# A fused attention and mixture kernel: first attention with two row tiles, joined latent weights, and the output's moments by the aggregate instruction

## The chip, the cores and the metric

One core of one Trainium2 chip runs the whole program in one launch. The metric is the device time of one execution in microseconds (us). TensorE is written PE (PEld is its weight load), VectorE DVE, ScalarE ACT, GpSimd POOL, SyncE SP. SBUF is the memory beside the engines, PSUM the one that PE writes, here 8 banks of 512 float32 columns.

## What is computed

All arrays are float32. Over 32 entries of 128 tokens x 128 features (x) with 120 context rows each, five stages run one after the other:

```
1 l0 attention: kv_in = [LN(ctx); LN(x)] (248 rows), q = LN(x) Wq, k,v = kv_in Wkv   (8 heads of 64)
                q, k are divided by their length per head; masked softmax of 8 q.k; y = (p v) Wo
                x = x + LN(y) w + b
2 l0 ffn:       up to three steps relu(x Wm^T) * active, Wp^T, with a choice of 512 columns between steps
3 l1 attention: 16 heads of 8, keys and values from ctx (120 rows)
4 mla:          16 heads of 8: q = h Wq, c = h Wdkv (64 wide), k = c Wuk, v = c Wuv, causal softmax, Wo
5 moe:          8 experts, the best two per token, silu(t w1) w2
```

## The kernel before, in words

Each stage is a function with one program per engine; engines meet only at semaphores, and each engine works off its own list in order. In the attention stages every engine runs a `body(n)` for each entry n, in which the work of entries n-1, n, n+1 and n+2 is interleaved by hand. That order is all there is of a schedule.

Stage 1 is `l0_attention`, with `softmax_units` for its softmax: eight heads are handled as two units u of four heads; a unit's scores fill two PSUM banks (2u and 2u+1), two heads of 248 columns in each. The steps of one entry m:

- DVE normalizes x and ctx (L650, L652), PE turns both (L474, L475), ACT copies them into `kvT`. PE projects q, kc (keys of ctx) and kl (keys of x) (L481, L482, L487); ACT copies each into `qk` (L586) and squares all (L591); DVE sums the squares (L657, L662); POOL takes the power -1/2 (L742, `r_norm`) and multiplies (L745, `qkn`). That POOL product is signalled as `normed`.
- PE turns `qkn` (L494, L498, L504); ACT and DVE copy it to `KT` and `QZ`. `QZ` holds, for each head, a 128-row tile of which 64 rows stay zero, so that a product over all 128 rows gives the score of one head (L384). The mask enters each bank as a product of `first_row` and `keep_row` (L380).
- DVE takes the maximum (L162), ACT the exponentials (L171), PE turns the probabilities (L184, L190), ACT and DVE copy them (L196, L201). DVE inverts the sums (L177) and spreads them (L414, `r_wide`), PE turns them (L421), ACT copies them (L428). PE multiplies by the values (L436, L438), DVE scales (L447), PE projects (L453), ACT copies `y` (L606).
- For y, DVE takes statistics (L675) and six small operations (L678 to L687), POOL the power (L751), DVE normalizes (L692), POOL weighs, biases and adds (L755 to L760), DVE takes the statistics of x (L697).

`copy_qk(m)` on ACT may overwrite `qk` only when `normed` has counted entry m-1, so the chain copies, kl projection, copy, squares, sums, power, product closes on itself once per entry. In bodies, `copy_qk(n + 2)` follows the exponentials of unit 1 of entry n.

In the mla stage (`attention16`, kind mla), PE makes the 64-wide latent c (L1405), ACT copies it (L1510), and PE makes keys and values from it (L1418, L1419), placed between `turn_group(n, par, 0)` and `turn_group(n, par, 1)`; `scores(n + 1)` (L1431 bias, L1436) come right after.

## Time and profile before

| | us |
|---|---|
| median of 3 runs | 1520.29 (1519.94 to 1520.65) |
| profiled execution, its own time | 1520.62 |
| its span, first to last instruction | 1518.9 |
| mean granted PE clock over the span | 0.942 of full speed |
| stage 1, to its last DVE row | 0 to 579.6 |
| stage 4 (mla) | about 1011 to 1266 |

Times in rows are us from the start of the span, except mean durations, which are in ns. The profile merges neighbouring instructions of a line ("x4"); a matmul of float32 is two instructions in the records, one for each part of the numbers.

### The profile page before, as it was taken

The page shows a single profiled execution, that of the slowest core. Times are in us where ns is not written, and L with a number is a line of the kernel's source. Part 1 is how long each engine was busy: PE and PEld are TensorE (multiplying, and loading weights), DVE is VectorE, ACT ScalarE, POOL GpSimd, SP SyncE. Part 2 cuts the span into 40 slices and gives each one's busy share as a digit, 9 for nine tenths or more (in the row PEclk, how much of TensorE's full clock was granted, in tenths as well). Part 3 has the DMA queues.
Part 4 walks back from the last instruction along what each step waited for, and adds up shares of the span by engine and source line. Part 5 has one row for each costly group of instructions (what it writes and reads, how often), then busy time and mean ns, then how long its engine had stood idle before and what let it go on. Part 6 is the DMA issues. An engine that isn't in the chain of part 4 may idle for free. (4 is left out here: it accounts for less than half of the span.)

```text
span 1518.9 us, 38140 instructions
## 1 busy us (share of the span) xinstructions
PE 1320.3 (87%) x13781; PEld 963.8 (63%) x13781; DVE 1031.7 (68%) x2266; ACT 759.3 (50%) x2067; POOL 559.6 (37%) x546
## 2 busy tenths in 40 slices
PE   1699999999999996931389988969999997999998
PEld 0377676776776773421277676747878885777776
DVE  5377777777777773767388888868999995343432
ACT  1467767767767661300155555536666663333332
POOL 3556555555555543000221222234222222334333
PEclk9899999999999997965599999988999998999999
DMA  7000000000000000000000000010000000000000
GB/s 200 0 1 0 0 0 0 0 0 0 0 0 0 0 1 0 0 1 0 9 11 7 8 8 8 7 57 2 1 0 0 0 2 1 8 8 14 7 7 14
DMA packets 22727, 14.56 MB, mean 10 GB/s; under 512 B 6377, under 2 KB 21609, under 8 KB 22538
## 3 DMA queue, kind: packets, MB, share of 16 engines
q1 hardware_dynamic: 22520, 13.75, 3.5%
q8 instruction: 37, 0.61, 0.2%
q14 instruction: 24, 0.20, 0.0%
q10 hardware_dynamic: 146, 0.01, 0.0%
HBM read 11.66 MB, written 2.10 MB: 9 GB/s over the span
## 5 line engine op out<-in xcount | busy, mean ns | idle before, releaser
L742 POOL TENSOR_TENSOR r_norm<-ssm,mhalf 128x24 f32<-128x24 f32 x32 | 133.6, 4176 | 176.1 <-DVE ssm L662 176.1
L171 ACT ACTIVATE l_probs<-psum,l_n_max 128x248 f32<-128x248 f32 x256 | 117.0, 481 | 101.4 <-DVE l_n_max L162 101.4
L1845 ACT ACTIVATE hid<-psum 128x512 f32<-128x512 f32 x128 | 76.3, 597 | 136.3 <-PE psum L1793 136.3
L1906 DVE TENSOR_TENSOR prod<-psum,combine 128x512 f32<-128x512 f32 x64 | 44.2, 691 | 143.9 <-PE psum L1803 143.9
L1803 PEld LDWEIGHTS psum<-w,hid 128*128 128x128 f32 x1024 | 123.1, 192 | 26.8 <-issue 26.8
L1937 POOL TENSOR_TENSOR acc<-acc,prod 128x512 f32<-128x512 f32 x64 | 81.1, 1268 | 146.9 <-DVE prod L1906 146.9
L384 PE MATMUL psum<-KT,QZ 128*128 128x248 f32 x512 | 128.4, 373 | 0.0
L1803 PE MATMUL psum<-w,hid 128*128 128x128 f32 x1024 | 123.4, 275 | 0.0
L1793 PE MATMUL psum<-moe_hT,w 128*128 128x512 f32 x256 | 122.0, 605 | 0.0
L384 PEld LDWEIGHTS psum<-KT,QZ 128*128 128x128 f32 x512 | 98.1, 192 | 18.9 <-issue 0.7
L1658 POOL TENSOR_TENSOR l_QX<-l_qT,l_own_slots 128x512 f32<-128x512 f32 x32 | 33.3, 1040 | 185.1 <-ACT l_qT L1504 178.5
L745 POOL TENSOR_TENSOR qkn<-qk,r_norm 128x1536 f32<-128x1536 f32 x32 | 88.4, 2762 | 3.6 <-POOL r_norm L742 2.2
L1658 POOL TENSOR_TENSOR mla_QX<-mla_qT,mla_own_slots 128x512 f32<-128x512 f32 x32 | 33.3, 1040 | 149.5 <-ACT mla_qT L1504 149.5
L1380 ACT COPY l_probsT<-psum 120x512 f32<-120x512 f32 x64 | 37.5, 585 | 100.4 <-PE psum L1446 100.4
L162 DVE TENSOR_REDUCE l_n_max<-psum 128x4 f32<-128x992 f32 x64 | 75.7, 1183 | 8.8 <-PE psum L384 8.8
L1446 PE MATMUL psum<-ident,mla_probs 128*128 128x128 f32 x512 | 76.2, 283 | 1.5 <-ACT mla_probs L1524 1.3
L657 DVE TENSOR_REDUCE ss<-sq 128x24 f32<-128x1536 f32 x32 | 56.1, 1753 | 30.1 <-ACT sq L591 30.1
L1524 ACT ACTIVATE mla_probs<-psum,mla_n_max 128x128 f32<-128x128 f32 x256 | 69.5, 382 | 13.9 <-DVE mla_n_max L1558 13.9
L201 DVE COPY l_probsT<-psum 128x512 f32<-128x512 f32 x64 | 43.9, 685 | 41.6 <-PE psum L190 41.6
L1446 PE MATMUL psum<-ident,l_probs 128*120 128x128 f32 x512 | 70.5, 281 | 0.0
L1524 ACT ACTIVATE l_probs<-psum,l_n_max 128x120 f32<-128x120 f32 x256 | 68.0, 385 | 5.0 <-DVE l_n_max L1558 5.0
L586 ACT COPY qk<-psum 128x512 f32<-128x512 f32 (+1 forms) x96 | 54.5, 619 | 30.6 <-PE psum L487 22.7
(307 smaller groups left out, 3458.8 us busy)
## 6 DMA issues: line engine op xcount, KB each, us to landing
X<-x_in SPq DMA_DIRECT2D x8, 256.0 KB, 4.9
out_dram<-acc SPq DMA_DIRECT2D x32, 64.0 KB, 1.5
CT<-ctx_in SPq DMA_DIRECT2D x8, 240.0 KB, 6.2
l_cT<-ctxT_in SPq DMA_DIRECT2D x32, 60.0 KB, 1.8
w<-w_in SPq DMA_DIRECT2D x1, 1024.0 KB, 4.9
wm<-wm_in SPq DMA_DIRECT2D x1, 768.0 KB, 4.6
wp<-wp_in SPq DMA_DIRECT2D x1, 768.0 KB, 6.7
wkv<-wkv_in SPq DMA_DIRECT2D x1, 512.0 KB, 5.1
```

What stands on the lines that cost most here:

```text
L162: dve.tensor_reduce(n_max[u][:, :].rearrange("p (c j) -> p c j", c=2), psum[:, 2 * u:2 * u + 2, 0:HB * K].rearrange("p c (j k) -> p c j k" ...
L171: e = act.activation(probs[u][:, h, :], psum[:, 2 * u + h // HB, (h % HB) * K:(h % HB + 1) * K], ACT.Exp, bias=n_max[u][:, h:h + 1], accum ...
L384: mm = pe.matmul(psum[:, 2 * u + c, j * K:(j + 1) * K], QZ[par][:, h, :], KT[par][:, h // 2, :], start=False, stop=True, skip_group_check= ...
L742: pool.tensor_tensor(r_norm[:, :], ssm[:, :], mhalf[:, 0:3 * H], ALU.pow).then_inc(s["norm_inverted"], 1)
L745: pool.tensor_tensor(qkn[:, :, :].rearrange("p a (h d) -> p (a h) d", d=HD), qk[:, :, :].rearrange("p a (h d) -> p (a h) d", d=HD), r_norm ...
L1446: tr = pe.transpose(psum[0:K, 4 + g % 2, j * P:(j + 1) * P], probs[par][:, 4 * g + j, :], ident[:, :])
L1524: e = act.activation(probs[par][:, h, :], psum[:, h // 4, (h % 4) * K:(h % 4 + 1) * K], ACT.Exp, bias=n_max[par][:, h:h + 1])
L1658: pool.tensor_tensor(QX[par][:, :, :], qT[:, :].unsqueeze(1).broadcast_to([P, 4, P]), own_slots[:, :].unsqueeze(2).broadcast_to([P, 4, P]) ...
L1793: pe.matmul(psum[:, 2 + i % BANKS, :], w1[:, e, half * P:(half + 1) * P], hT[par][:, :], start=True, stop=True).then_inc(hidden[i], 1)
L1803: mm = pe.matmul(psum[:, 5 + e % 2, b * D:(b + 1) * D], hid[i % RING][:, b * P:(b + 1) * P], w2[:, i, :], start=(half == 0), stop=(half == ...
L1845: act.activation(hid[i % RING][:, :], psum[:, 2 + i % BANKS, :], ACT.Silu).then_inc(activated[i], 1)
L1937: pool.tensor_tensor(a[:, :, :], a[:, :, :], prod[e % 2][:, :, :], ALU.add).then_inc(summed[e], 1)
```

## The change

It has five parts.

1. Stage 1, scores: q is kept compact in `QT` (64 rows for each head, two heads above each other), and two heads are multiplied at a time, one on array rows 0 to 63 and one on 64 to 127, each into its own bank. The mask is given at rows 0 and 64, from a small tile `keep_now` that POOL copies for each entry. The value products are written down in another order (context part of two heads, then x part of the two).
2. Stage 1, order: `softmax_units` and `run_entries` go, and every engine gets a new `body`, run by `run_steps` from n = -2 to 33 (a step is skipped where its entry does not exist). The old bodies are printed above, the new ones stand in the diff.
3. Stage 1, moments of y: `bn_aggr` gives mean and variance at once, and one addition of epsilon follows.
4. Stage 1, scales of the later entries (two powers over 28 columns each, L119) are cut into four pairs over 7 columns.
5. Stage 4: Wdkv Wuk and Wdkv Wuv are multiplied once in the stage's setup (`joined`), and q, k, v come straight from the input in one step `project_qkv`. Stage 3 gets the same step with its own weights.

```diff
-        QZ = [sb(f"QZ{i}", [P, H, P]) for i in range(2)]
+        QT = [sb(f"QT{i}", [P, 4, P]) for i in range(2)]
+        keep_now = [sb(f"keep_now{i}", [P, K], BF16) for i in range(2)]
...
-                act.dma_start(keep8[:, :], keep_in).then_inc(keep_loaded, 16)
+                for r in (0, 64):
+                    act.dma_start(keep8[r:r + 1, :], keep_in).then_inc(keep_loaded, 16)
...
-                dve.tensor_scalar(keep_row[0:1, :, 0:C], keep8[:, :].rearrange("a (b c) -> a b c", b=B), 1.0, -NEG_MAX,
-                                  ALU.subtract, ALU.mult)
+                for r in (0, 64):
+                    dve.tensor_scalar(keep_row[r:r + 1, :, 0:C], keep8[r:r + 1, :].rearrange("a (b c) -> a b c", b=B), 1.0, -NEG_MAX,
+                                      ALU.subtract, ALU.mult)
...
-            dst, src = QZ[par][r, half:H:2, :], psum[r, 7, :].rearrange("p (c q) -> p c q", c=4)
+            dst, src = QT[par][r, :, :], psum[r, 7, :].rearrange("p (c q) -> p c q", c=4)
...
-            pe.matmul(psum[:, 2 * u + c, 0:2 * K], first_row[:, :], keep_row[:, entries(n), :].broadcast_to([P, 2, K]),
-                      start=True, stop=False, skip_group_check=True)
-            for j in range(2):
-                h = 4 * u + 2 * c + j
-                mm = pe.matmul(psum[:, 2 * u + c, j * K:(j + 1) * K], QZ[par][:, h, :], KT[par][:, h // 2, :],
-                               start=False, stop=True, skip_group_check=True)
...
+                def scores(n, u, par):
+                    if there(n):
+                        if u == 0:
+                            wait(pe, s["qT_copied"], n + 1)
+                            wait(pe, s["qT_scaled"], n + 1)
+                            wait(pe, s["klT_copied"], n + 1)
+                            wait(pe, s["keep_copied"], n + 1)
+                        wait(pe, exp_done[u], n)
+                        for r in range(2):
+                            pe.matmul(psum[:, 2 * u + r, 0:2 * K], first_row[64 * r:64 * r + 64, :],
+                                      keep_now[par][64 * r:64 * r + 64, :].unsqueeze(1).broadcast_to([64, 2, K]),
+                                      start=True, stop=False, skip_group_check=True)
+                        for j in range(2):
+                            for r in range(2):
+                                mm = pe.matmul(psum[:, 2 * u + r, j * K:(j + 1) * K], QT[par][64 * r:64 * r + 64, 2 * u + j, :],
+                                               KT[par][64 * r:64 * r + 64, 2 * u + j, :], start=False, stop=True,
+                                               skip_group_check=True)
+                        mm.then_inc(scored[u], 1)
...
-            for j in range(4):
-                h = 4 * u + j
-                o = psum[HD * (j % 2):HD * (j % 2) + HD, 5, (j // 2) * P:(j // 2 + 1) * P]
-                pe.matmul(o, VC[par][0:C, h * HD:(h + 1) * HD], probsT[u][0:C, 0, j, :], start=True, stop=False,
-                          skip_group_check=True)
-                mm = pe.matmul(o, VL[par][:, h * HD:(h + 1) * HD], probsT[u][:, 1, j, :], start=False, stop=True,
-                               skip_group_check=True)
-            mm.then_inc(pv_done[u], 1)
...
+                        for j in range(2):
+                            for part, V, rows in ((0, VC, C), (1, VL, P)):
+                                for r in range(2):
+                                    h = 4 * u + 2 * j + r
+                                    mm = pe.matmul(psum[HD * r:HD * r + HD, 5, j * P:(j + 1) * P], V[par][0:rows, h * HD:(h + 1) * HD],
+                                                   probsT[u][0:rows, part, 2 * r + j, :], start=(part == 0), stop=(part == 1),
+                                                   skip_group_check=True)
+                        mm.then_inc(pv_done[u], 1)
...
+                def body(n, par):
+                    values_x(n + 1)
+                    scores(n, 1, par)
+                    project(n - 1)
+                    turn_inputs(n + 2)
+                    turn_probs0(n, 0)
+                    turn_probs1(n, 0)
+                    project_kc(n + 2)
+                    turn_sums(n, 0)
+                    project_q(n + 2)
+                    multiply_v(n, 0, par)
+                    turn_probs0(n, 1)
+                    turn_kc(n + 1)
+                    project_kl(n + 2)
+                    turn_probs1(n, 1)
+                    turn_kl(n + 1)
+                    turn_q(n + 1)
+                    multiply_v(n, 1, par)
+                    turn_sums(n, 1)
+                    values_c(n + 2)
+                    scores(n + 1, 0, 1 - par)
...
+                def copy_part(m, part, proj, copied, bank, rows):
+                    if there(m):
+                        wait(act, s["normed"], m)
                         wait(act, s[proj], m + 1)
-                        act.copy(qk[0:rows, i, :], psum[0:rows, bank, :]).then_inc(s[copied], 1)
...
+                def body(n, par):
+                    copy_values_c(n + 1, 1 - par)
+                    exponentials(n, 0)
+                    take_projection(n - 1)
+                    make_kvT(n + 2)
+                    copy_pt0(n, 0)
+                    copy_values_x(n + 1, 1 - par)
+                    exponentials(n, 1)
+                    copy_sums(n, 0)
+                    copy_part(n + 2, 1, "kc_proj", "kc_copied", 6, C)
+                    copy_part(n + 2, 0, "q_proj", "q_copied", 7, P)
+                    copy_pt0(n, 1)
+                    copy_kcT(n + 1, 1 - par)
+                    copy_part(n + 2, 2, "kl_proj", "kl_copied", 7, P)
+                    square_qk(n + 2)
+                    copy_qT(n + 1, 1 - par)
+                    copy_sums(n, 1)
...
-                    dve.tensor_tensor(y_sums[:, :], y_stat[:, 1:3], y_stat[:, 4:6], ALU.add)
-                    dve.tensor_tensor(y_diff[:, :], y_stat[:, 1:2], y_stat[:, 4:5], ALU.subtract).then_inc(s["y_aggr"], 1)
-                    wait(dve, s["y_aggr"], n + 1)
-                    dve.tensor_scalar(y_mean[:, :], y_sums[:, 0:1], 0.5, None, ALU.mult)
-                    dve.tensor_scalar(y_within[:, :], y_sums[:, 1:2], 1.0 / D, LN_EPS, ALU.mult, ALU.add)
-                    dve.scalar_tensor_tensor(y_between[:, :], y_diff[:, :], 0.25, y_diff[:, :], ALU.mult,
-                                             ALU.mult).then_inc(s["y_parts"], 1)
-                    wait(dve, s["y_parts"], n + 1)
-                    wait(dve, s["y_inverted"], n)
-                    dve.tensor_tensor(y_var[:, :], y_within[:, :], y_between[:, :], ALU.add).then_inc(s["y_var_ready"], 1)
...
+                        wait_apart(dve, s["y_stats"], n + 1, s["ln_made"])
+                        dve.bn_aggr(y_moment[:, :], y_stat[:, :]).then_inc(s["y_aggr"], 1)
+                        wait(dve, s["y_aggr"], n + 1)
+                        wait(dve, s["y_inverted"], n)
+                        dve.tensor_scalar(y_var[:, :], y_moment[:, 1:2], LN_EPS, None, ALU.add).then_inc(s["y_var_ready"], 1)
...
+                def body(n, par):
+                    norm_inputs(n + 2)
+                    maximum(n, 1)
+                    invert_sums(n, 0)
+                    y_moments(n - 1)
+                    copy_pt1(n, 0)
+                    scale_out(n, 0)
+                    invert_sums(n, 1)
+                    copy_pt1(n, 1)
+                    copy_kl(n + 1, 1 - par)
+                    copy_qT(n + 1, 1 - par)
+                    sum_squares(n + 2)
+                    y_normalize(n - 1)
+                    maximum(n + 1, 0)
+                    scale_out(n, 1)
+                    x_moments(n - 2)
...
+                def copy_keep(m, par):
+                    if there(m):
+                        wait(pool, scored[1], m - 1)
+                        pool.tensor_copy(keep_now[par][:, :], row(keep_row, m)).then_inc(s["keep_copied"], 1)
...
+                def body(n, par):
+                    weigh(n - 2)
+                    copy_keep(n + 2, par)
+                    invert_deviation(n - 1)
+                    add_to_x(n - 2)
+                    invert_norms(n + 2)
+                    norm_qk(n + 2)
+                    later_scales(n)
...
+            wdkvT = sb("wdkvT", [LAT, D])
+            joined = sb("joined", [D, 2, D])
+            w_turned, w_copied, w_joined = sem("w_turned"), sem("w_copied"), sem("w_joined")
         with nc.Block() as block:
+            if not l1:
+                @block.tensor
+                def _(pe):
+                    pe.transpose(psum[0:LAT, 6, 0:D], wdkv[:, :], ident[:, :]).then_inc(w_turned, 1)
+                    pe.wait_ge(w_copied, 1)
+                    pe.matmul(psum[:, 7, 0:D], wdkvT[:, :], wk[:, :], start=True, stop=True)
+                    pe.matmul(psum[:, 7, D:2 * D], wdkvT[:, :], wv[:, :], start=True, stop=True).then_inc(w_joined, 1)
+                @block.scalar
+                def _(act):
+                    act.wait_ge(w_turned, 1)
+                    act.copy(wdkvT[:, :], psum[0:LAT, 6, 0:D]).then_inc(w_copied, 1)
+                    act.wait_ge(w_joined, 1)
+                    act.copy(joined[:, :, :], psum[:, 7, 0:2 * D].rearrange("p (w d) -> p w d", w=2))
...
-                def project_q(m):
+                def project_qkv(m, par):
                     if there(m):
                         wait(pe, z_copied, m + 1)
-                        if not l1:
-                            pe.matmul(psum[0:LAT, 7, 2 * P:3 * P], wdkv[:, :], zT[:, :], start=True, stop=True)
-                        pe.matmul(psum[:, 7, P:2 * P], wq[:, :], zT[:, :], start=True, stop=True).then_inc(q_proj, 1)
-                def project_kv(m, par):
-                    if there(m):
                         if l1:
                             wait(pe, c_loaded[par], (m - par) * 8 + 16)
-                            source = cT[par]
-                        else:
-                            wait(pe, lat_copied, m + 1)
-                            wait(pe, q_copied, m + 1)
-                            source = latT
-                        at = 2 * P if l1 else 0
-                        pe.matmul(psum[:, 7, at:at + K], wk[:, :], source[:, :], start=True, stop=True)
-                        pe.matmul(psum[0:K, 7, 3 * P:4 * P], source[:, :], wv[:, :], start=True, stop=True).then_inc(kv_proj, 1)
+                        pe.matmul(psum[:, 7, P:2 * P], wq[:, :], zT[:, :], start=True, stop=True)
+                        source = cT[par] if l1 else zT
+                        pe.matmul(psum[:, 7, 2 * P:2 * P + K], wk[:, :] if l1 else joined[:, 0, :], source[:, :], start=True, stop=True)
+                        pe.matmul(psum[0:K, 7, 3 * P:4 * P], source[:, :], wv[:, :] if l1 else joined[:, 1, :],
+                                  start=True, stop=True).then_inc(qkv_proj, 1)
                 def scores(n, par):
...
-                    project_q(n + 1)
+                    project_qkv(n + 1, 1 - par)
                     for g in range(4):
                         multiply_v(n - 1, 1 - par, g)
                     turn_group(n, par, 0)
-                    project_kv(n + 1, 1 - par)
                     turn_group(n, par, 1)
...
-                    copy_latent(n + 1)
```

## Rows read from the trace of the kernel before

**Rows 1.** Windows: busy PE, PEld, DVE, ACT, POOL, clock, DMA share, GB/s.

```profile
200.00:300.00 100.00, 99.87 (x634) 70.00 (x634) 73.28 (x160) 69.76 (x196) 54.14 (x39) 1.00 0.00 0
```

**Rows 2.** Timeline of PE and ACT in stage 1: start, duration, line, shape.

```profile
319.89 0.38 PE L380 MATMUL psum<-keep_row,first_row 128*128 x1
320.12 1.00 PE L384 MATMUL psum<-KT,QZ 128*128 128x248 f32 x4
...
323.50 0.47 ACT L171 ACTIVATE l_probs<-psum,l_n_max 128x248 f32<-128x248 f32 x1 [3.12 <-DVE l_n_max L162]
...
324.09 1.05 PE L453 MATMUL psum<-wo,outT 128*128 128x128 f32 x8
...
325.28 0.28 ACT L606 COPY y<-psum 128x128 f32<-128x128 f32 x1
...
328.10 0.45 PE L436 MATMUL psum<-l_probsT,VC 120*64 120x128 f32 x4
...
329.18 1.12 PE L481 MATMUL psum<-wq,kvT 128*128 128x512 f32 x2
```

**Rows 3.** Timeline of POOL, second and last product (29 entries apart).

```profile
83.93 2.76 POOL L745 TENSOR_TENSOR qkn<-qk,r_norm 128x1536 f32<-128x1536 f32 x1
...
553.27 2.76 POOL L745 TENSOR_TENSOR qkn<-qk,r_norm 128x1536 f32<-128x1536 f32 x1
```

**Rows 4.** Timeline from one product to the next power.

```profile
72.08 1.07 ACT L586 COPY qk<-psum 128x512 f32<-128x512 f32 x2 [3.18 <-POOL qkn L745]
...
73.88 0.58 ACT L586 COPY qk<-psum 128x512 f32<-128x512 f32 x1 [0.73 <-PE psum L487]
74.31 0.69 DVE L201 COPY l_probsT<-psum 128x512 f32<-128x512 f32 x1 [2.12 <-PE psum L190]
...
76.12 1.50 ACT L591 ACTIVATE sq<-qk 128x1536 f32<-128x1536 f32 x1
77.65 1.75 DVE L657 TENSOR_REDUCE ss<-sq 128x24 f32<-128x1536 f32 x1 [0.79 <-ACT sq L591]
...
79.69 4.16 POOL L742 TENSOR_TENSOR r_norm<-ssm,mhalf 128x24 f32<-128x24 f32 x1 [7.65 <-DVE ssm L662]
```

**Rows 5.** The page's costliest groups: busy us, mean ns, idle before.

```profile
L162 DVE TENSOR_REDUCE l_n_max<-psum 128x4 f32<-128x992 f32 x64 | 75.7, 1183 | 8.8 <-PE psum L384 8.8
```

**Rows 6.** DVE beside the POOL product of a later entry.

```profile
326.79 2.76 POOL L745 TENSOR_TENSOR qkn<-qk,r_norm 128x1536 f32<-128x1536 f32 x1 [0.16 <-POOL r_norm L742]
...
327.56 0.28 DVE L675 BATCH_NORM_STATS2 y_stat<-y 128x6 f32<-128x128 f32 x1
327.87 1.69 DVE L678 TENSOR_TENSOR y_sums<-y_stat 128x2 f32<-128x2 f32 x1
```

**Rows 7.** Instructions of two tiles: count, min/median/max ns, first and last start.

```profile
L414 DVE COPY r_wide<-l_r_sums x64: 293/294/2789, 65.6 to 570.7; 128x256 f32<-128x256 f32 x64
...
L1865 DVE TENSOR_SCALAR hn<-X,rms x32: 273/276/1326, 1271.9 to 1466.1; 128x128 f32 x24, 128x128 f32<-128x128 f32 x8
```

**Rows 8.** Timeline of PE in one mla entry.

```profile
1150.92 1.17 PE L1436 MATMUL psum<-mla_kT,mla_QX 32*128 32x128 f32 x32
...
1152.03 0.49 PE L1466 MATMUL psum<-mla_wo,mla_outT 128*128 128x128 f32 x2
...
1152.46 1.04 PE L1446 MATMUL psum<-ident,mla_probs 128*128 128x128 f32 x8
...
1153.43 0.43 PE L1405 MATMUL psum<-mla_zT,mla_wdkv 128*64 128x128 f32 x2
```

**Rows 9.** Longest waits in mla, 1060 to 1240: total, times, longest.

```profile
DVE mla_n_max L1558 <- PE psum L1436: 8.5, 24, 0.4
```

**Rows 10.** Setup, first entry and end of stage 1.

```profile
21.13 2.14 DVE L331 TENSOR_SCALAR keep_row<-keep 1x3840 bf16<-1x3840 uint8 x1
...
41.09 2.76 POOL L745 TENSOR_TENSOR qkn<-qk,r_norm 128x1536 f32<-128x1536 f32 x1
...
579.34 0.29 DVE L697 BATCH_NORM_STATS2 stats<-X 128x6 f32<-128x128 f32 x1 [1.70 <-POOL X L760]
```

More of the change, by code:

```diff
@@ L220, in l0_attention, with there @@
+def there(n):
+    return not isinstance(n, int) or 0 <= n < B
 def l0_attention(nc, psum, X, stats6, mean, rstd, mhalf, small, ident, ident_bf, ones, cols,
@@ new lines, in project @@
+                def project(n):
+                    if there(n):
+                        wait(pe, out_scaled[1], n + 1)
+                        for c in range(4):
+                            mm = pe.matmul(psum[:, 5, 0:D], outT[:, c, :], wo[:, c, :], start=(c == 0), stop=(c == 3))
+                        mm.then_inc(s["projected"], 1)
+                def body(n, par):
[19 more added lines that the diff above has]
+                    scores(n + 1, 0, 1 - par)
@@ L578, in make_kvT @@
-                    act.activation(kvT[:, C:K], psum[:, 6, P:2 * P], ACT.Identity, bias=LNL_B,
-                                   scale=LNL_W).then_inc(s["kvT_made"], 1)
-                def copy_qk(m):
-                    wait(act, s["normed"], m)
-                    for i, (proj, copied, bank, rows) in enumerate((("q_proj", "q_copied", 7, P), ("kc_proj", "kc_copied", 6, C),
-                                                                    ("kl_proj", "kl_copied", 7, P))):
+                    if there(m):
+                        wait(act, s["ln_turned"], m + 1)
+                        wait(act, s["vc_proj"], m)
+                        wait(act, s["vl_proj"], m)
+                        act.activation(kvT[:, 0:C], psum[:, 6, 0:C], ACT.Identity, bias=LNX_B, scale=LNX_W)
+                        act.activation(kvT[:, C:K], psum[:, 6, P:2 * P], ACT.Identity, bias=LNL_B,
+                                       scale=LNL_W).then_inc(s["kvT_made"], 1)
@@ new lines, in exponentials @@
+                def exponentials(n, u):
+                    if there(n):
+                        wait(act, max_taken[u], n + 1)
+                        wait(act, pt1_turned[u], n)
+                        wait(act, pt0_turned[u], n)
+                        wait(act, sum_inverted[u], n)
+                        for h in range(4):
+                            e = act.activation(probs[u][:, h, :], psum[:, 2 * u + h // 2, (h % 2) * K:(h % 2 + 1) * K], ACT.Exp,
+                                               bias=n_max[u][:, h:h + 1], accum_out=sums[u][:, h:h + 1])
+                        e.then_inc(exp_done[u], 1)
```

662 lines of the change are left out of this document (259 added, 403 removed).

## The prediction, written before the changed kernel was run

> **What bounds the kernel now.** I read the windows first. In stage 1 PE is recorded busy 99.87 us of 100 while ACT, DVE and POOL have 70, 73 and 54 [rows 1]. In mla DVE waits for nothing but 0.35 us of scores an entry (8.5 us in 24) [rows 9], so there it is DVE that is near its limit. The timeline of stage 1 then gives the period of an entry: the POOL product starts at 83.93 and, 29 entries later, at 553.27 [rows 3], so one entry takes 469.34 / 29 = 16.18 us. The reader should see in it which work PE spends: the scores of an entry run from 319.89 to 324.09, 4.2 us, four banks of 1.05 [rows 2]. So a cut of PE's work moves the period, until another chain sets it. The first product starts at 41.09 [rows 10], 42.8 us before the second; two periods would be 32.4, so 10.5 us are lost in the start. Stage 1 ends at 579.6 [rows 10].
>
> **Scores on two row tiles.** A bank costs a mask of 0.23 us (320.12 - 319.89) and four records of two heads, (1.05 - 0.23) / 4 = 0.21 each [rows 2]. If the two tiles run together, a unit costs 0.23 + 4 x 0.21 = 1.07 instead of 2.10. That they do run together is shown in mla: 32 records of 128 columns on four row tiles take 1152.03 - 1150.92 = 1.11 us, while eight transposes of 128 columns one after the other take 1153.43 - 1152.46 = 0.97, so 0.11 to 0.12 each [rows 8]; 32 in turn would need 3.5. The switch of tile shape costs something: eight records at 0.11 are 0.87, the next shape starts at 0.97, so 0.1 is left for a switch. Each of the two units now stands between full-array work on both sides, four switches, 0.4. PE saves 4.2 - 2 x 1.07 - 0.4 = 1.7 us an entry. The Trainium skill (TensorEngine Tiling (Array Packing), Tiling Modes, Key Properties) says that a change of tiling mode drains the engine; by that rule four more drains speak against the change, and this trace agrees on a cost, of about 0.1 us. By a free switch the saving would be 2.1, by the row 1.7. Bounds: no overlap at all gives -0.4 (a loss), full overlap with free switches 2.1; I take 1.7, since the mla row is the same kind of product.
>
> **Value products.** Sixteen records of 128 columns take 329.18 - 328.10 = 1.08 us [rows 2], where one after the other at 0.11 they would take 1.76. They overlap already, and the new writing order brings 0, at best 1.08 - 0.9 = 0.2 a unit.
>
> **What PE's own list then allows.** 16.18 - 1.7 = 14.5 us if all its present gaps stay, about 13.7 if the gaps of some 0.8 us close (my estimate from a walk along the list). Now the other chains count, and the new order decides them.
>
> **The chain of the norms.** ACT may copy `qk` only after `normed` of the entry before. In the new order it is: the product ends, ACT copies kc and q (1.07 for two), projection of kl until its copy starts (73.88 - 72.66 = 1.2, where 72.66 is the end of the first of the two copies), copy 0.58, squares 1.50, sums and the clamp until the power starts 79.69 - 77.65 = 2.04 [rows 4], power to product 4.34, product 2.76 [rows 6]. That is 13.5; DVE takes the turned q ahead of the sums (0.25), signals 0.1: 13.9 us. The closed chain is a floor that the old order did not reach.
>
> **ACT's list.** From the copy of kc: 4.4 us to the end of the squares (1.07 + 1.2 + 0.58 + 1.50), DVE's sums and clamp to 6.7, y normalized and the maximum of unit 0 (1.18 [rows 5]) to 8.2. Then four exponentials take 325.28 - 323.50 = 1.78 [rows 2], to 10.0, y copied at 10.5 once PE has projected (0.28 [rows 2]), then two halves of kvT, two copies like that of kl, exponentials 1.78 and the copied sums, together 3.8 by my estimate: 14.3 us until kc can be copied again. Without further trouble the period is max(13.7 to 14.5, 13.9, 14.3) = 14.3.
>
> **The port that DVE and POOL share.** While the product runs on POOL, some DVE operations stand still. `y_sums` starts at 327.87 and ends with the product at 329.55, taking 1.69 instead of 0.16 [rows 6]; `r_wide`, a copy inside SBUF, once took 2789 ns instead of 294, and `hn`, a multiplication by a scale, 1326 instead of 276 [rows 7]. The statistics of y, started at 327.56 in the midst of it, took their usual 0.28 [rows 6]. So a DVE operation with two SBUF inputs, or a simple SBUF copy or scaling, waits until the product ends; statistics do not. By the list above, DVE reaches the moments of y at about 11.3 of a period, and the product runs from 11.1 to 13.85: inside. `bn_aggr` I take as free like the statistics (0.2). The last step, the addition of epsilon to a 128x1 column, is a tensor_scalar from SBUF to SBUF, the form of `hn`. Its cost is between 0.15 and the rest of the product, 2.4. The nearest row says that it waits, and I take that. The Trainium skill (SBUF — State Buffer, which ops grab the shared pair) lists tensor_scalar among the operations that may take two ports; whether one with a single element per partition does, no row here shows.
>
> What is late next: `copy_pt1(n, 0)` is queued behind it on DVE, PE waits with the value products of unit 0, and behind those, in order, stand the turn of unit 1's probabilities, the turn of kc and the projection of kl. The chain closes through the product: copy 0.69 [rows 4], values 1.08 [rows 2], eight transposes 0.88 [rows 8], projection 1.2, copy 0.58, squares 1.50, sums 2.04 [rows 4], power 4.34, product 2.76 [rows 6], with five signals of about 0.1: **15.5 us**. ACT's list and PE's list fit into that.
>
> **Moments of y, masks, scales.** Five small DVE operations go, besides the wait in `y_sums`, off the path. POOL copies a mask of 248 columns each entry; its product over 1536 columns takes 2.76 [rows 6], so that is well under 1 us, and POOL is idle 46% of the time [rows 1], mostly ahead of the power: 0. The powers over 28 columns leave the start; the first interval becomes about one period. The setup gets a second `keep_row` operation of 2.14 us on DVE [rows 10], of which 0.4 to 2.1 is seen, and kc is projected ahead of q (0.9): the first product ends near 45.9 instead of 43.85. After the last product (556.0) 23.6 us follow today; 21.5 by the shorter list.
>
> Stage 1 then ends at 45.9 + 31 x 15.5 + 21.5 = 547.9, that is 31.7 us less.
>
> **Joined latent weights.** PE loses the latent product (two records, about 0.35 us [rows 8]) and two changes of tile shape, 0.5 in all; ACT loses a copy. The scores can start 0.5 earlier. DVE waits for them 0.35 us an entry [rows 9] and has no other gap, so the gain ends there: 31 x 0.3 = 9 us, from 0 to 11. The joint weights are made on idle PE and ACT beside 5 us of DVE work in the setup: 0; uncovered it would be 3. Stage 3 changes by 0: its PE asks for the same data in nearly the same order.
>
> **Sum.** 1518.9 - 31.7 - 9 = 1478.2 of span. The profiled execution took 1520.62, 1.7 more than its span and 0.3 more than the median; so 1478.2 + 1.7 - 0.3 = 1479.6, **1480 us**. Its own range is 1470 to 1490 (15.2 to 15.8 us an entry).
>
> **Rivals.**
> - *The small addition does not wait for the port.* Period 14.3: stage 1 ends at 45.9 + 443.3 + 21.5 = 510.7, so 68.9 + 9 less: **1442 us**. For it: one element per partition gains nothing from two ports. Against: `y_sums`, two elements, waited. With 13.9 to 14.8 it is 1430 to 1458.
> - *The row tiles do not overlap, or the parts of the float32 products run in turn.* PE has then 16.18 + 0.4, less gaps of 0.8: about 15.9. Stage 1 ends at 560, **1492 us**. The change would not do what it says, and the new order alone would pay. The mla row speaks against it. The same time comes if `r_wide` of unit 0, 0.4 us ahead of the product in my walk, slips behind its start.
> - *Slower.* The lock puts the whole product on the path: `r_wide` waits from its start, PE stands at `turn_sums`, and nothing behind it makes the time up. The period is 14.3 + 2.76 = 17.1, stage 1 ends at 597, **1529 us**. It decides from a period of (579.6 + 9 - 45.9 - 21.5) / 31 = 16.8 on. Against it: PE has other work to catch up with.
> - *Mla gains nothing* is inside each range (9 us).
>
> **Chances.** Addition waits 0.48, does not wait 0.34, no overlap or a late `r_wide` 0.11, slower 0.05, no change 0.02. The range 1434 to 1500 holds the first wholly, nearly all of the second and the third. Faster by over 0.2% is 0.93, within 0.2% (3 us, about what a measurement of this kernel can tell from none) 0.02, slower 0.05.
>
> **What would show it.** The spacing of the L745 products: 15.5, against 14.3 and 15.9. The duration of the small addition after `bn_aggr`: over 1 us or 0.15. The start of neighbouring score records: in pairs, and a unit of about 1.1 us. In mla, the wait of the maximum for PE: near 0, and a period shorter by 0.3. The prediction is wrong if DVE reaches the moments outside of the product, or if a chain that I did not walk (the first exponentials behind the sums on DVE) is longer than its rows.

## The result and the profile after

| | before | after |
|---|---|---|
| median | 1520.39 us (4 runs, 1519.94 to 1520.65) | 1445.07 us (4 runs, 1443.46 to 1447.12) |
| span of the profiled execution | 1518.9 | 1445.4 |
| stage 1 ends | 579.6 | 515.5 |
| two entries of mla, start to start | 14.70 | 13.79 |

The ratio is 0.9506, 95% interval 0.9489 to 0.9522: faster by 75 us. That lies in the predicted range (1434 to 1500), but not in the likeliest case (1480, itself 1470 to 1490). It is the first rival, "the small addition does not wait for the port", which gave 1442. The two profiled spans differ by 73.5 us: 64.1 in stage 1, 15 in mla, and the other stages together 5.6 longer in this execution.

Of the 64 us in stage 1, 51.6 are the period (29 entries of 1.78 us). Another 13.8 lie between the first POOL product and the third (42.8 us before, 29.0 after), against a first product that comes 2.3 us later. The prediction expected that first gain too. All runs below that start from the changed kernel keep most of it, so a run with nearly the old period can still be faster than the kernel before: old_order is by 25 us, 15 of them in mla. No run takes the new start back alone.

The timeline of POOL, third and last product of the changed kernel, 29 entries apart (against [rows 3]):

```profile
72.41 2.76 POOL L691 TENSOR_TENSOR qkn<-qk,r_norm 128x1536 f32<-128x1536 f32 x1
...
490.14 2.76 POOL L691 TENSOR_TENSOR qkn<-qk,r_norm 128x1536 f32<-128x1536 f32 x1
```

One entry takes (490.14 - 72.41) / 29 = **14.40 us**, where it took 16.18. The windows of 200 to 300 us, columns as in [rows 1]:

```profile
200.00:300.00 100.00, 99.95 (x722) 64.83 (x722) 69.94 (x145) 79.20 (x215) 62.94 (x50) 1.00 0.00 0
```

PE has almost no recorded gap (99.95 us busy of 100), as before; ACT does more in the same time (79 against 70 us). DVE has fewer busy us per 100 (70 against 73) although more entries pass: the wait inside `y_sums` and the small operations behind it are gone. The timeline of POOL and DVE shows the disputed addition (L645):

```profile
302.86 2.76 POOL L691 TENSOR_TENSOR qkn<-qk,r_norm 128x1536 f32<-128x1536 f32 x1
...
302.96 0.18 DVE L642 BATCH_NORM_AGGREGATE y_moment<-y_stat 128x2 f32<-128x6 f32 x1
303.18 0.15 DVE L645 TENSOR_SCALAR y_var<-y_moment 128x1 f32<-128x1 f32 x1
303.26 0.69 DVE L626 COPY l_probsT<-psum 128x512 f32<-128x512 f32 x1
```

DVE does reach the moments inside the product, as the walk said. But the addition takes 0.15 us there and the copy of unit 0's probabilities follows at once. In [rows 6] `y_sums` stood until the product's end.

The timeline of PE, the two units of scores around the value projection:

```profile
311.97 0.38 PE L386 MATMUL psum<-keep_now,first_row 64*128 64x496 bf16 x2
312.19 1.00 PE L391 MATMUL psum<-KT,QT 64*128 64x248 f32 x8
313.12 1.12 PE L375 MATMUL psum<-wkv,kvT 128*128 128x512 f32 x2
314.18 0.38 PE L386 MATMUL psum<-keep_now,first_row 64*128 64x496 bf16 x2
...
315.33 1.16 PE L444 MATMUL psum<-wo,outT 128*128 128x128 f32 x8
316.32 0.27 PE L322 MATMUL psum<-ident,ln_c 120*128 120x120 f32 x1
```

A unit takes 313.12 - 311.97 = 1.15 us with its switch (2.10 in [rows 2]): the row tiles run side by side.

### The profile page after: what moved, and what is told of

It reads as the page before. It is cut to its first block and busy times, and to the rows that moved or that the text cites. A ratio compares the mean times of both kernels' runs of the same rounds, so it can differ in the third digit from the quotient of the medians.

```text
span 1445.4 us, 38156 instructions
## 1 busy us (share of the span) xinstructions
PE 1241.4 (86%) x13722; PEld 888.8 (61%) x13722; DVE 974.8 (67%) x2140; ACT 766.0 (53%) x2037; POOL 569.5 (39%) x582
## 5 line engine op out<-in xcount | busy, mean ns | idle before, releaser
L634 DVE TENSOR_TENSOR outT<-psum,r_spread 128x256 f32<-128x256 f32 x64 | 26.9, 420 | 78.8 <-PE psum L435 73.3
L1396 PE MATMUL psum<-ident,mla_probs 128*128 128x128 f32 x512 | 69.8, 280 | 1.2 <-ACT mla_probs L1465 1.0
L1733 PEld LDWEIGHTS psum<-moe_hT,w 128*128 128x128 f32 x256 | 45.3, 195 | 35.8 <-issue 35.3
L1339 DVE COPY mla_probsT<-psum 128x512 f32<-128x512 f32 x96 | 62.8, 682 | 2.3 <-PE psum L1396 2.3
```

Of the source, the lines that this page charges most:

```text
L1339: copy(probsT[0:K, g, :, :], psum[0:K, 4 + g % 2, :].rearrange("k (j q) -> k j q", j=4)).then_inc(copied[g], 1)
L1396: tr = pe.transpose(psum[0:K, 4 + g % 2, j * P:(j + 1) * P], probs[par][:, 4 * g + j, :], ident[:, :])
L1733: pe.matmul(psum[:, 2 + i % BANKS, :], w1[:, e, half * P:(half + 1) * P], hT[par][:, :], start=True, stop=True).then_inc(hidden[i], 1)
```

## The experiments

Each changes one thing in the changed kernel, but for one that starts from the kernel before. The period is that of the POOL products, over 28 or 29 entries. Differences in us are to 1445.07.

| run | time, us | ratio to before (interval) | period, us |
|---|---|---|---|
| changed kernel | 1445.07 | 0.9506 (0.9489 to 0.9522) | 14.40 |
| old_order | 1495.72 | 0.9832 (0.9812 to 0.9853) | 16.11 |
| full_array | 1505.38 | 0.9892 (0.9875 to 0.9909) | 16.24 |
| old_moments | 1494.98 | 0.9829 (0.9811 to 0.9848) | 16.10 |
| two_elements | 1476.07 | 0.9699 (0.9683 to 0.9715) | 15.37 |
| two_late | 1446.80 | 0.9511 (0.9495 to 0.9527) | 14.40 |
| before_aggregate | 1521.44 | 1.0003 (0.9993 to 1.0012) | 16.18 |
| old_mla | 1460.59 | 0.9605 (0.9589 to 0.9621) | 14.41 |
| pe_less | 1432.63 | 0.9418 (0.9403 to 0.9434) | 14.08 |
| act_less | 1443.78 | 0.9490 (0.9474 to 0.9506) | 14.37 |
| scores_pair | 1458.76 | 0.9593 (0.9577 to 0.9609) | 14.83 |
| short_mask | 1443.57 | 0.9498 (0.9483 to 0.9514) | 14.38 |
| pe_swap | 1435.83 | 0.9447 (0.9434 to 0.9460) | 14.10 |

### The addition over two elements, and where it stands

```diff
-dve.tensor_scalar(y_var[:, :], y_moment[:, 1:2], LN_EPS, None, ALU.add)
+dve.tensor_scalar(y_var[:, :], y_moment[:, 0:2], LN_EPS, None, ALU.add)   # y_var is [P, 2]
```

> The changed kernel with the addition of epsilon written over two elements per partition (mean and variance, of which only the second is used) instead of one. Theory A, an operation of one element per partition needs no second port and one of two elements does: the addition stands from about 0.3 us after the start of POOL's product to its end, 2.4 us instead of 0.15; by the prediction's chain the period is then 15.5 us and the time 1445 + 31 x 1.1 = 1479 us. Theory B, such a small scaling by constants never waits: 0.15 us, 14.4 us, 1445 us. Theory C, it waits but the wait is hidden: 2.4 us, and 1445 to 1452 us.

The timeline of POOL and DVE of that kernel:

```profile
301.67 2.76 POOL L691 TENSOR_TENSOR qkn<-qk,r_norm 128x1536 f32<-128x1536 f32 x1
...
302.17 2.29 DVE L645 TENSOR_SCALAR y_var<-y_moment 128x2 f32<-128x2 f32 x1
304.37 0.68 DVE L626 COPY l_probsT<-psum 128x512 f32<-128x512 f32 x1
```

The addition ends at 304.46, within 0.03 us of the product's end (304.43). Its mean over 24 entries is 2.38 us, against 0.154 with one element. The period is 15.37 and the time 1476, where theory A said 15.5 and 1479. So the chain that the prediction walked for its main case was right to 0.13 us; only its premise was not met. The same kernel with the moments moved:

```diff
                     invert_sums(n, 0)
-                    y_moments(n - 1)
                     copy_pt1(n, 0)
                     scale_out(n, 0)
+                    y_moments(n - 1)
```

> The kernel with the addition over two elements, and the three operations on the moments of y moved on DVE from ahead of the copy of unit 0's turned probabilities to behind the scaling of unit 0's output, which starts after POOL's product has ended. Theory A, the addition over two elements waits for the product and for nothing else: 0.15 us, period 14.4 us, 1445 us (up to 1452 if the later statistics delay POOL's power for y). Theory B, the operation over two elements is slow wherever it stands, or something else than the product holds it: 2.3 us, period 15.4 us, 1476 us.

The groups of instructions, 100 to 470 us (busy us, mean ns of one, idle before), first of the kernel with two elements, then of this one:

```profile
L645 DVE TENSOR_SCALAR y_var<-y_moment 128x2 f32<-128x2 f32 x24 | 57.1, 2377 | 2.1
```

```profile
L645 DVE TENSOR_SCALAR y_var<-y_moment 128x2 f32<-128x2 f32 x26 | 4.4, 170 | 2.2
```

The same instruction takes 0.17 us once it starts behind the product, and the time is that of the changed kernel again. It is the product that holds it, and only where it has two elements. (The edit also starts the source at the first column instead of the second; no run separates that from the count.)

### The three parts of stage 1, each taken back alone

old_moments restores `y_sums` and the five small operations behind it:

```diff
-                        dve.bn_aggr(y_moment[:, :], y_stat[:, :]).then_inc(s["y_aggr"], 1)
+                        dve.tensor_tensor(y_sums[:, :], y_stat[:, 1:3], y_stat[:, 4:6], ALU.add)
...
```

> The changed kernel with the six small DVE operations for the moments of the output in place of the aggregate instruction and the addition. The first of them has two inputs in SBUF and waited for POOL's product in the kernel before. Theory A, the prediction's chain was right and only its premise (that the addition waits) was wrong: the wait of 2.4 us is back, period 15.5 us or more, 1479 us or more. Theory B, the wait is covered by other work on PE and ACT: the first operation takes 2.4 us, but the period stays under 14.8, 1445 to 1457 us.

The timeline of POOL and DVE:

```profile
296.90 2.76 POOL L701 TENSOR_TENSOR qkn<-qk,r_norm 128x1536 f32<-128x1536 f32 x1
...
297.01 2.67 DVE L646 TENSOR_TENSOR y_sums<-y_stat 128x2 f32<-128x2 f32 x1
299.60 0.15 DVE L647 TENSOR_TENSOR y_diff<-y_stat 128x1 f32<-128x1 f32 x1
...
300.34 0.68 DVE L630 COPY l_probsT<-psum 128x512 f32<-128x512 f32 x1
```

`y_sums` ends with the product (299.66), and the copy starts 0.68 us after it; in two_elements it started 0.06 ahead of it. The periods differ by the same amount, 0.73 us (16.10 - 15.37). Theory A's period of "15.5 or more" holds, and the five small operations cost what they take, since they stand on the chain too. The prediction had them at nothing.

old_order puts the four lists back. The core, on ACT (the order of copies before and after):

```diff
-copy_part(kc) copy_part(q) copy_pt0(n, 1) copy_kcT copy_part(kl) square_qk copy_qT copy_sums(n, 1)
+copy_part(q) copy_part(kc) copy_part(kl) copy_pt0(n, 1) copy_kcT copy_qT copy_sums(n, 1) square_qk exponentials(n + 1, 0)
```

> The changed kernel with the four lists of stage 1 put back into the order of the kernel before (copies, products and DVE operations as there; the row tiles, the small masks, the aggregate instruction and the joined weights stay). Theory A, the tiles are what pays and PE's list is the bound: PE had no recorded idle time in either order, so the period is 16.18 - 1.8 = 14.4 us as after, and only the start is longer by some us: 1445 to 1455 us. Theory B, the order is what let the period follow PE's work: in the old order the closed chain of the norms (product, copies, projection of kl, squares, the four exponentials, sums, power, product) holds at 15 to 15.6 us, so 1465 to 1485 us.

Neither number was met: the period is 16.11. That the order holds the period is theory B, its size is not, and neither is the chain that it names. The timeline from product to product:

```profile
299.54 2.76 POOL L691 TENSOR_TENSOR qkn<-qk,r_norm 128x1536 f32<-128x1536 f32 x1
...
303.67 1.11 ACT L498 COPY qk<-psum 128x512 f32<-128x512 f32 x2
...
305.57 0.59 ACT L498 COPY qk<-psum 128x512 f32<-128x512 f32 x1 [0.79 <-PE psum L339]
...
307.82 1.50 ACT L506 ACTIVATE sq<-qk 128x1536 f32<-128x1536 f32 x1
...
311.22 1.18 DVE L607 TENSOR_REDUCE l_n_max<-psum 128x4 f32<-128x992 f32 x1
311.39 4.18 POOL L684 TENSOR_TENSOR r_norm<-ssm,mhalf 128x24 f32<-128x24 f32 x1 [4.73 <-DVE ssm L589]
312.44 0.47 ACT L527 ACTIVATE l_probs<-psum,l_n_max 128x248 f32<-128x248 f32 x1 [3.13 <-DVE l_n_max L607]
312.79 1.16 PE L444 MATMUL psum<-wo,outT 128*128 128x128 f32 x8 [1.74 <-DVE outT L634]
314.85 0.58 ACT L477 COPY VC<-psum 120x512 f32<-120x512 f32 x1 [0.34 <-PE psum L368]
...
315.65 2.76 POOL L691 TENSOR_TENSOR qkn<-qk,r_norm 128x1536 f32<-128x1536 f32 x1
```

The product ends at 302.30, and ACT comes to the copies of `qk` only at 303.67, behind the exponentials, without a wait. So power and product have 1.4 us to spare and do not close this loop; in the kernel before it was the same (product's end 329.55 [rows 6]). The row of the copies there:

```profile
330.97 1.12 ACT L586 COPY qk<-psum 128x512 f32<-128x512 f32 x2
```

What ACT waits for is the maximum (3.13 us), which stands behind the sums of the squares on DVE, and then PE, whose projection of the output waits 1.74 us for the scaling behind that maximum. By these rows the loop that closes at 16.11 is copies, projection of kl, squares, sums, maximum and scaling, exponentials and the projection of the output, values, exponentials of unit 1, copies. In it four other copies stand ahead of the squares (306.16 to 307.82, 1.7 us lost), and the new order takes them out of there. PE's recorded busy time is 89.1 us of 100 here, and the period is still 16.1. The members of the loop are read from the rows; the run shows that the order as a whole sets the period.

full_array gives the scores their full array back:

```diff
-QT[par][64 * r:64 * r + 64, 2 * u + j, :], KT[par][64 * r:64 * r + 64, 2 * u + j, :]
+QZ[par][:, 4 * u + 2 * j + r, :], KT[par][:, 2 * u + j, :]
```

> The changed kernel with the scores on the full array again, from queries padded with zeros in half of the rows; new order, masks of 248 columns, aggregate instruction and joined weights stay. A unit of scores then takes 2.1 us instead of 1.15. Theory A, PE's list is the bound and order alone brings nothing: period 14.4 + 2 x 0.95 = 16.3 us, 31 x 1.9 = 59 us more, 1504 us. Theory B, the order brings a good part: period 15.0 to 15.6, 1464 to 1482 us.

Theory A: 16.24 us and 1505 (16.3 and 1504 expected), with PE busy 99.24 of 100. Last, the aggregate instruction alone in the kernel before:

> The kernel before with the aggregate instruction and one addition in place of its six small operations for the moments of the output, and nothing else changed. Theory A, three limits of almost the same length held the old period: PE's list (16.2, seen with scores on the full array in the new order), the norms' chain of the old order (16.1, seen with the old order and everything else new) and the port wait; taking one away brings nothing: 16.1 to 16.2 us, 1515 to 1521 us. Theory B, the wait of 1.7 us and the five operations behind it were on the path on their own: the period falls by 0.5 to 1.7 us, 1468 to 1505 us.

Nothing moves (1.0003, interval 0.9993 to 1.0012). Taken together: with all three parts 14.40; without the order 16.11, without the tiles 16.24, without the aggregate 16.10; with none 16.18, with the aggregate alone 16.18. Two limits of nearly one length held the old kernel, PE's list and the loop of the old order, and taking away one leaves the other. By the lists, the port is a third only beside the new order: that order has `y_moments` ahead of `copy_pt1(n, 0)` on DVE, so that PE's value products wait for it. In the old order it stood behind that copy, and taking its wait of 1.6 to 1.7 us away changed nothing. two_late says that a moments step behind the scaling costs nothing even in the new order, so moving the six old operations there might have done instead of the aggregate; no run tests that.

### What holds 14.40

pe_less leaves out two of the four chunks of the projection, act_less the fourth exponential of unit 1:

```diff
-                        for c in range(4):
+                        for c in range(2):
```

> The changed kernel with two of the four chunks of the output projection of stage 1 left out, so four of eight records and 0.5 us of PE's work less in an entry (the output of stage 1 lacks the heads of the other chunks). Theory A, PE's list sets the period of 14.40 us: it falls by about 0.5, to 13.9, 1430 us. Theory B, ACT's list (closed over the exponentials, the copies, the squares, the sums and the maximum on DVE) sets it: it falls by 0.0 to 0.15, 1440 to 1445 us.

```diff
-                        for h in range(4):
+                        for h in range(4 - u):
```

> The changed kernel with the fourth exponential of unit 1 left out in stage 1 (0.45 us of ACT's work less in an entry; that head's probabilities are constants). Theory B, ACT's list sets the period of 14.40 us: it falls by 0.4 or until the norms' chain (13.9) or PE's list meets it, 13.95 to 14.1, 1431 to 1436 us. Theory A, PE's list sets it: it falls by 0.0 to 0.1, 1442 to 1445 us.

Half a microsecond less on PE gives 0.32 an entry (12.4 us in all); 0.45 less on ACT gives 0.03 (1.3 us, which the two intervals do not tell from nothing). So PE's list holds 14.40. The timelines say what stands at 14.08. First ACT's copy of `y` and the copies of `qk` in the changed kernel, then in pe_less the first exponential, the same two and PE's turning of the probabilities:

```profile
316.60 0.27 ACT L547 COPY y<-psum 128x128 f32<-128x128 f32 x1 [0.23 <-PE psum L444]
...
320.44 1.14 ACT L498 COPY qk<-psum 120x512 f32<-120x512 f32 x2
```

```profile
308.27 0.47 ACT L527 ACTIVATE l_probs<-psum,l_n_max 128x248 f32<-128x248 f32 x1 [1.73 <-DVE l_n_max L607]
...
310.06 0.27 ACT L547 COPY y<-psum 128x128 f32<-128x128 f32 x1
310.23 0.66 PE L401 MATMUL psum<-ident,l_probs 128*120 128x128 f32 x4 [0.17 <-ACT l_probs L527]
...
313.92 1.13 ACT L498 COPY qk<-psum 120x512 f32<-120x512 f32 x2
```

From the first exponential of unit 0 (314.47 in the changed kernel) to `y` it is 316.60 - 314.47 = 2.13 us there and 310.06 - 308.27 = 1.79 in pe_less: ACT no longer waits for the projection, and this 0.34 is the whole gain. From there to the next squares ACT takes 7.0 us in both, and in pe_less it is now PE that waits for the exponentials (0.17). So what stands at 14.08 is ACT's own list, closed over sums and maximum on DVE, which the prediction walked to 14.3. The product ends 0.08 us before the copies there (313.84) and lies close behind, but ACT does not wait for it. That is read from rows; no run shortens ACT and PE together.

### A shorter list on PE

```diff
 (scores_pair, PE)
+                    scores(n, 1, par)
+                    values_c(n + 1)
                     values_x(n + 1)
-                    scores(n, 1, par)
...
-                    values_c(n + 2)
                     scores(n + 1, 0, 1 - par)
```

> The changed kernel with the scores of both units next to each other on PE (both value projections behind them), ACT's copy of the values of the context behind the exponentials of unit 0, and y normalized behind the maximum on DVE. PE saves the two changes of tile shape between the units, 0.1 us each. Theory A, PE's list sets the period and nothing else is close: 14.4 - 0.2 = 14.2 us, 1439 us. Theory B, the later copy of the values holds up the turned inputs on PE, or the maximum of unit 0 comes later into the list: 14.4 to 14.8 us, 1445 to 1457 us.

Slower by 13.7 us: theory B, a little beyond its range (14.83 and 1459, where it said up to 14.8 and 1457). The timeline of ACT in this kernel:

```profile
302.28 1.48 ACT L506 ACTIVATE sq<-qk 128x1536 f32<-128x1536 f32 x1 [0.17 <-ACT qk L498]
...
307.24 0.47 ACT L527 ACTIVATE l_probs<-psum,l_n_max 128x248 f32<-128x248 f32 x1 [2.55 <-DVE l_n_max L607]
...
309.03 0.59 ACT L477 COPY VC<-psum 120x512 f32<-120x512 f32 x1
```

and of the changed kernel:

```profile
309.18 1.48 ACT L506 ACTIVATE sq<-qk 128x1536 f32<-128x1536 f32 x1 [0.17 <-ACT qk L498]
...
312.15 0.59 ACT L477 COPY VC<-psum 120x512 f32<-120x512 f32 x1 [0.56 <-PE psum L368]
...
314.47 0.47 ACT L527 ACTIVATE l_probs<-psum,l_n_max 128x248 f32<-128x248 f32 x1 [1.73 <-DVE l_n_max L607]
```

From the squares to the first exponential it is 4.96 us against 5.29, the 0.3 that the earlier maximum gives. But from there to the next squares it is 14.76 - 4.96 = 9.80 against 14.40 - 5.29 = 9.11. The copy of the values, 0.59 us, stood in ACT's wait for the maximum and cost nothing; behind the exponentials it is part of ACT's closed list, and the turned inputs on PE wait for it (2.8 us in 7 entries, a wait that the changed kernel hasn't). 0.69 - 0.33 = 0.36 is the rise in this entry. Entries of 14.76 and 14.92 alternate here, so the mean rises by 0.42; the other 0.16 of every second entry is not broken down.

short_mask puts the mask products last and over the context's columns alone. It doesn't compute the same scores (in each bank two products now set `start=True`, where one did); the amount of work is as described.

```diff
-mask, 496 columns, start=True;  then scores start=False
+scores, start=True;  then mask, 2 x 120 columns, start=False
```

> The changed kernel with the mask products behind the scores and over the 2 x 120 columns of the context alone (the 2 x 128 columns of the inputs get a zero today), so 240 columns instead of 496 a bank. PE saves 0.1 us a unit, by 0.21 us for 496 columns. Theory A, PE's list sets the period: 14.2 us, 1439 us. Theory B, the mask products run beside the start of the scores today and cost less than their record, or the changed order costs a switch of its own: 14.3 to 14.4 us, 1442 to 1445 us.

The timeline of PE:

```profile
309.54 1.11 PE L387 MATMUL psum<-KT,QT 64*128 64x248 f32 x8
310.48 0.27 PE L391 MATMUL psum<-keep_now,first_row 64*128 64x240 bf16 x2
310.68 1.13 PE L375 MATMUL psum<-wkv,kvT 128*128 128x512 f32 x2
```

Theory B: the period stays at 14.38. The pair of masks takes 310.68 - 310.48 = 0.20 us over 240 columns, where it took 312.19 - 311.97 = 0.22 over 496, but it now stands ahead of the change of tile shape, which costs the record ahead of it 0.09 (below). And the scores take 0.94, with the same tile shape behind them, where pe_swap has 0.84. So fewer columns may well save 0.1, and the changed order costs that back; the run doesn't separate the two. A unit is 1.14 us, and was 1.15.

pe_swap exchanges two steps and moves nothing else:

```diff
+                    scores(n, 1, par)
                     values_x(n + 1)
-                    scores(n, 1, par)
```

> The changed kernel with one pair exchanged in PE's list of stage 1: the scores of unit 1 stand directly behind those of unit 0, and the value projection of the inputs behind both. Nothing is moved on the other engines. PE saves two changes of tile shape, 0.1 us each by the trace, and the maximum of unit 0 still finds its scores at the same time. Theory A, PE's list sets the period: 14.4 - 0.2 = 14.2 us, 1445 - 6 = 1439 us. Theory B, another chain stands directly behind PE's list (with half a microsecond less on PE the period fell by 0.32 alone), or the later value projection delays ACT's copies: 14.3 to 14.5 us, 1442 to 1448 us.

1435.83 us against 1445.07, and the intervals of the two ratios (0.9434 to 0.9460, 0.9489 to 0.9522) don't meet: this version beats both kernels. The timeline of PE:

```profile
306.75 0.38 PE L386 MATMUL psum<-keep_now,first_row 64*128 64x496 bf16 x2
306.97 1.00 PE L391 MATMUL psum<-KT,QT 64*128 64x248 f32 x8
307.81 0.37 PE L386 MATMUL psum<-keep_now,first_row 64*128 64x496 bf16 x2
308.01 1.00 PE L391 MATMUL psum<-KT,QT 64*128 64x248 f32 x8
308.94 1.12 PE L375 MATMUL psum<-wkv,kvT 128*128 128x512 f32 x2
309.91 1.05 PE L444 MATMUL psum<-wo,outT 128*128 128x128 f32 x8
310.80 0.27 PE L322 MATMUL psum<-ident,ln_c 120*128 120x120 f32 x1
```

With the same tile shape behind them, unit 0's score records last 307.81 - 306.97 = 0.84 us, with another shape 0.93. Two units and the value projection take 3.16 us here and 315.33 - 311.97 = 3.36 in the changed kernel. The record behind a change is longer too: the output's projection takes 310.80 - 309.91 = 0.89 us behind the same shape, and 316.32 - 315.33 = 0.99 behind scores. Together PE's list is 0.30 shorter (4.05 against 4.35 us for the stretch), and the period falls by 0.30. So the two changes that were taken out cost 0.15 each, not 0.1. It ends at 14.10, by pe_less at 14.08, where ACT's list stands.

### The mla stage

old_mla takes the whole function of stages 3 and 4 from the kernel before.

> The changed kernel with the function of the mla stage of the kernel before (latents of their own, no joined weights); stage 1 as changed. Theory A, the joined weights account for the whole shortening of mla: two entries take 14.70 us again instead of 13.79, and the time is 1445 + 15 = 1460 us. Theory B, the sum of the prediction (0.3 us an entry, 9 in all) was right and the rest came from elsewhere: 1454 us. Stage 1's period stays 14.4 us in both.

15.5 us more than the changed kernel, theory A. The timeline of DVE, first with the old function, then with the joined weights:

```profile
1053.18 0.28 DVE L1543 BATCH_NORM_STATS2 stats<-X  x1
1053.82 1.23 DVE L1500 TENSOR_REDUCE mla_n_max<-psum 128x8 f32<-128x1024 f32 x1 [0.36 <-PE psum L1378]
```

```profile
1050.10 0.28 DVE L1541 BATCH_NORM_STATS2 stats<-X  x1
1050.30 1.21 DVE L1498 TENSOR_REDUCE mla_n_max<-psum 128x8 f32<-128x1024 f32 x1
```

From start to start it is 0.64 us with the wait and 0.20 without: 0.44 saved, where the wait is recorded as 0.36. An instruction that need not wait starts 0.08 us before the record of the one ahead of it ends, and a wait loses that overlap as well. The period is 0.455 shorter, which is 14 us in 31 entries; the rest of the 15 lies ahead of the first entry's output.

## Why the prediction was right in its range and wrong in its likeliest case

- **The failed step** is in the part on the shared port: "The nearest row says that it waits, and I take that." The addition over 128x1 took 0.154 us in the middle of the product, not up to 2.4. The nearest rows had two and 128 elements a partition, and the property that decides was the count. The rival's own argument, "one element per partition gains nothing from two ports", was the right one, and two_elements and two_late bear it out. The Trainium skill (VectorE: DVE Perf Modes, Mode 2×_2P) lets a DVE operation with one source read the two halves of its data through both ports, and asks that the outermost dimension other than 1 be even (or odd and equal in source and destination). The measurements agree with a reading in which a single element has no such dimension and no halves: 2.38 us for 128x2, 0.154 for 128x1. The prediction had weighed only the list in the Trainium skill (SBUF — State Buffer, which ops grab the shared pair), where tensor_scalar is among the operations that may take two ports.
- **The chain behind the lock** was right: 15.5 foretold, 15.37 measured with the lock brought back.
- **Scores on row tiles**: a unit 1.07 and a switch 0.1 foretold. Without a switch behind it a unit is 0.22 + 0.84 = 1.06, so that was right; a switch costs 0.15 (pe_swap). The saving foretold was 1.7 us an entry. The stretch from the context's value projection to the turned inputs takes 316.32 - 311.02 = 5.3 us, and 6.8 in full_array: 1.5 saved. The period falls by 1.84 between the two, so 0.3 of it comes from elsewhere, which isn't broken down.
- **PE's list** (14.5 with its gaps, 13.7 without): it is the limit, at 14.40. The gaps closed by about 0.1 only. **ACT's list**, on which the rival's 14.3 rested, is not the limit; by the rows of pe_less it is the next one, at about 14.1. The rival's number was met by another list than the one named, which is luck for the number: 1445 against 1442.
- **The rival "no overlap"** had the new order alone pay down to 15.9: without the tiles it is 16.24, so order alone pays nothing in the period.
- **The old order**: the text has its limits as PE's list alone. The loop through squares, sums, maximum and the first exponentials was as long (16.11): in the old order, tiles and aggregate together gain 0.07 us an entry. The prediction named the first exponentials behind the sums as a chain that it had not walked; in the old order that chain decides. "The closed chain is a floor that the old order did not reach" holds for the norms: they had 1.4 us to spare.
- **Moments of y**: the five small operations were taken as 0 beside the port. Taking the old moments back costs 50 us (1494.98 - 1445.07), 31 from the port's wait (two_elements) and 19 from the operations behind it.
- **Start and tail**: the first product ends at 46.16 (45.9 foretold); from the last product's end, 492.90, to the end of stage 1 it is 22.6 us (21.5 foretold).
- **Mla**: 9 us foretold, 15.5 measured. The place was right, the size was read from the recorded wait alone, 0.3 for 0.45 an entry.

## What to carry to other kernels

Before pricing a change that shortens one engine's list, close every other loop and compare, by following at each step what the engine really waits for (here copies, squares, sums, maximum, exponentials, copies; not the norms' product, which had 1.4 us to spare). If two are within 1%, neither pays alone, and an experiment that undoes one part says nothing of what that part is worth by itself. A new order can also put a wait on the path that was harmless before, as it did with the moments of y. A wait in front of a saturated engine costs its recorded idle time and the overlap with the instruction ahead. Where an operation of a new size is priced by its nearest row, ask which property of that row decides (elements per partition, not the operation's name).

## What the runs showed of the hardware

- A DVE tensor_scalar from SBUF to SBUF waits for a POOL product with SBUF inputs when it has two elements a partition (2.38 us) and not when it has one (0.154 us).
- `bn_aggr` over 128x6 takes 0.18 us when it starts in the product, and 0.18 behind it (two_late).
- A pair of bf16 mask products on two row tiles takes 0.22 us over 496 columns ahead of scores of the same tile shape, and 0.20 over 240 columns ahead of another shape.
- A change of tile shape on PE shows as 0.09 us on the score records ahead of it and 0.10 on the output's projection behind it; taking away two changes shortened the period by 0.30 us and gave 9 us in 32 entries.
- PE recorded 99.9 us of 100 busy in the kernel before, and another loop had nearly the same length (16.11 of 16.18 us); with that loop alone (old_order) PE recorded 89.1.
